# Sorting 200,000 edges in groups of eight tiles: lookup tables by groups of four nodes, one lookup product and sum a group, key rows by broadcast DMA

## The chip, the cores and the metric

The kernel runs on one core of a Trainium2 chip. Times are microseconds (us) on the device for one execution. The time of a kernel is the median of its runs: 11170.59 us here, of three runs between 11164.8 and 11173.62.

## What is computed

Two graph layers stand behind each other on 12,500 nodes with 32 features and 200,000 edges, `src` to `dst`, sorted by `dst` as they come in. The first is a spline convolution whose edge coordinates are moved by a small network (two more spline convolutions, of ones and of 64 hidden features) before it is applied to the features. The second is graph attention with four heads and a GRU cell. Cut to the order of the work:

```python
h = jnp.maximum(_layernorm(x), 0.0)
row, col = src, dst
msg = einsum('es,eso->eo', basis, z[col[:, None] * K + idx])   # K = 125, S = 8
out = segment_sum(msg, row) / max(segment_sum(ones, row), 1) + b
new_pseudo = clip(pseudo + t[col] - t[row], 0, 1)              # t from two such convolutions
x = x + spline_conv(h, row, col, *spline_basis(new_pseudo), W, b)
h = jnp.maximum(_layernorm(x), 0.0)
alpha = softmax over the edges into dst of leaky_relu(el[src] + er[dst])
x = x + elu(GRU(segment_sum(feat[src] * alpha, dst), h))
```

The spline convolutions sum by `src`, so the edges are needed in the order of `src` too. The kernel sorts them itself. The change is in that sort.

## The kernel before

The program is written by hand, engine by engine. It runs through phases, each a block with one instruction stream for each of SP (SyncE, which only issues DMAs here), DVE, ACT, PE and POOL, with semaphores between them. On the profile's clock:

- `constants`, then `load_nodes_and_edges` (L150 to L217) up to 66 us: keys, edge coordinates and features come in. The keys lie as 128 partitions by 1568 tiles, so a **tile** is 128 edges, one a partition. DVE splits each `src` key into its low 7 bits `src_lo` and its high part `src_hi` (0 to 97), makes `c.src`, the key in f32, and builds the records (key, `dst`, three coordinates) that will be sorted.
- `count_and_prefix`, up to about 523 us: counts the edges of each node with one-hot products and makes `c.base`, where the edges of each node start in the sorted order, as a table of 128 (low part) by 98 (high part).
- `sort_edges` (L440 to L612), 524 to 3254 us: it works out the place of each edge and scatters its record there.
- the convolution of ones to about 4040 us, the one of hidden features, two passes of `flow_conv` to about 6600 and 9550 us, the second norm, and the attention to the end. POOL gathers rows by indirect DMAs in the flow phases too (L961, L1614), in steps of 128 rows.

**`sort_edges`** takes the 1568 tiles in 196 groups of G = 8. `u` is the parity of the group g and picks one of two buffers. The place of an edge is the number that stands for its key in the running table (where the next edge of this key goes), plus how many edges before it in its pair of tiles have the same key. For a group:

- DVE makes the one-hots of the *next* group: `rk_lo` (8 x 128, L463) and `rk_hi` (8 x 98, L465).
- PE transposes the eight `rk_lo` one-hots (`turn`, L522), and ACT copies them to SBUF as `rk_lo_t` (`take_lo`, L567).
- So that each edge can be compared with all edges of its pair of tiles, every partition needs the keys of a tile in a row. PE makes them: ACT copies the group's keys to `rk_cols` (L564), and `rows_of` multiplies them, broadcast over 128 columns, by the identity in f32 (L530), into `rk_rows_ps` in PSUM.
- PE goes through the tiles in four pairs, k = 0 to 3. Two products add the one-hots of the pair to the running table `rk_run_ps` in PSUM (L549, bf16, 98 columns). ACT copies it to `rk_table` (L587), in turn in two buffers. Two products look up the pair in the table as it was before the pair (L554, f32, 98 columns): they pick for each edge the row of its low part.
- For every tile, DVE counts the equal keys that stand earlier (L487, one instruction over 128 or 256 elements with a sum at its end). It then waits for the tile's lookup and picks the column of the high part by a product with `rk_hi` and a sum (L492). At the end of the group it adds the two (L497, `rk_place`).
- POOL waits for the place and for ACT's copy of the records (`rk_rec`, L583). It then issues eight indirect DMAs (L609, `rec<-rk_rec,rk_place`), one a tile, each of which writes 128 records of 32 bytes to their places.
- SP stores `feat_table` (L503), then clears `rows4` for a later phase by 112 DMAs of 252 KB each (L506, `rows<-rk_blank`), behind each other and without a wait.

What orders the work is the semaphores. DVE may write `place` when the scatters of group g-2 have landed (`scattered[u]`), ACT `rec` likewise. PE's lookup of tile j waits (L553) until DVE has taken tile j-2, which used the same half of `rk_look_ps`. DVE's one-hots for g+1 wait until PE has added the last pair of g-1, and `rows_of(g + 1)` is issued behind each pair of g. The two waits of DVE and of POOL that the scatters hang on:

```python
dve.wait_ge(looked, g * G + j + 1)                 # before L492, for every tile
...
pool.wait_ge(place_made, g + 3)
pool.wait_ge(rec_ready, g + 1)
```

Of the kernel before, what the change touches and what calls it, by code (L numbers as in the profile page):

```python
# [6 lines left out]
BF16 = mybir.dt.bfloat16  # L7
# [18 lines left out]
NQ = NW // G  # L26
SPREADS = 4
# [124 lines left out]
def load_nodes_and_edges(nc, c, d, sem):  # L152
# [4 lines left out]
    with nc.Block() as block, ExitStack() as ctx:  # L157
        sb, _, _ = allocators(nc, ctx)
        tmp, stat = sb("ln_tmp", [P, NB, FEAT]), sb("ln_stat", [P, 3, NB])
        pseudo = sb("pseudo", [P, NT, 3])  # L160
        keys_stored = sem("in_keys_stored")

        @block.sync
        def _(sp):
# [20 lines left out]
            sp.dma_start(d.dst_key.rearrange("(p t) w -> p (t w)", t=PIECES), c.dst_i[:, :]).then_inc(keys_stored, 16)  # L185
            sp.wait_ge(keys_stored, 32)

        @block.scalar
        def _(act):
            act.wait_ge(var_ready, 1)  # L190
            act.activation(stat[:, 2, :], stat[:, 1, :], ACT.Sqrt).then_inc(std_ready, 1)

        @block.vector
        def _(dve):
# [7 lines left out]
            for a in (c.src, c.src_lo, c.src_hi):  # L202
                chain(dve.memset(a[:, NT:NT + G], 0.0))
# [3 lines left out]
            chain(dve.tensor_copy(c.src[:, 0:NT], c.src_i[:, :]))  # L207
# [5 lines left out]
            chain(dve.tensor_copy(c.rec[:, :, 0:1], c.src[:, 0:NT].unsqueeze(2)))  # L213
# [7 lines left out]
def count_and_prefix(nc, c, d, sem):  # L221
# [6 lines left out]
    with nc.Block() as block, ExitStack() as ctx:  # L228
# [26 lines left out]
        def _(dve):  # L255
# [50 lines left out]
            chain(dve.tensor_copy(off[:, :], first))  # L306
            dve.sem_inc(off_made, 1)
# [111 lines left out]
def sort_edges(nc, c, d, sem):  # L419

    hots_made = sem("rk_hots_made")
    turned = sem("rk_turned")
    lo_ready = sem("rk_lo_ready")
    cols_made = sem("rk_cols_made")
    rows_made = sem("rk_rows_made")
# [3 lines left out]
    sums = sem("rk_sums")  # L433
# [3 lines left out]
    pool_turn = sem("rk_pool_turn")  # L437
    tail_made = sem("rk_tail_made")
    earlier_made = sem("rk_earlier_made")
    blank_made, blank_stored, feat_stored = sem("rk_blank_made"), sem("rk_blank_stored"), sem("rk_feat_stored")  # L440
    with nc.Block() as block, ExitStack() as ctx:
        sb, ps, _ = allocators(nc, ctx)
        lo_hot, hi_hot = sb("rk_lo", [P, 2, G, P], BF16), sb("rk_hi", [P, 2, G, NB], BF16)
        lo_t = sb("rk_lo_t", [P, 2, G, P])
        table = sb("rk_table", [P, 2, NB])
        junk, junk_l = sb("rk_junk", [P, 2, G // 2, 3, P], BF16), sb("rk_junk_l", [P, 2, G, NB], BF16)
# [7 lines left out]
        lo_ps = ps("rk_lo_ps", [P, G, P], BF16)
        rows = ps("rk_rows_ps", [P, 2, G, P])
        look = ps("rk_look_ps", [P, 2, 512])
        run = ps("rk_run_ps", [P, 512])
# [57 lines left out]
        def _(pe):  # L515
# [1476 lines left out]
```

## Time and profile before

| | |
|---|---|
| median of the runs | 11170.59 us (11164.8 to 11173.62) |
| span of the profiled execution | 12528.6 us; it has no time beside its span |
| PE, PEld busy | 6505.4 us (52%), 5397.9 us (43%) |
| DVE busy | 7716.2 us (62%) |
| ACT busy | 2933.1 us (23%) |
| POOL busy | 7476.5 us (60%) |
| DMA | 605.09 MB, 48 GB/s over the span |

The span runs from the first to the last instruction of one execution that the profiler recorded. A busy time is the sum of an engine's instructions. PEld is the loading of PE's weights, beside PE. L487 and the like are lines of the kernel, which stand above with their numbers. A wait is put down to the engine whose semaphore ended it; where the profile finds none, it says "remote" or "issue". One core runs, so nothing is remote in the sense of another core.

### The profile page before, as it was taken

How to read it: one execution, taken by the hardware profiler on the slowest of the kernel's cores; microseconds unless marked ns; L12 is line 12 of the kernel's file. 1: busy time of each engine (PE TensorE's matmuls, PEld its weight loads, DVE VectorE, ACT ScalarE, POOL GpSimd, SP SyncE). 2: the span in 40 equal slices, each digit the busy share in tenths (PEclk: the TensorE clock that was granted, in tenths of full speed). 3: DMA queues.
4: the chain of work that ended last, by engine and by line, in shares of the span. 5: the costliest groups of instructions: out<-in, count | busy, mean ns of one | idle time of the engine just before them, and what ended most of it. 6: DMA issues, size and time to landing. Idle time of an engine off the chain costs nothing. (4 is left out here: it accounts for less than half of the span.)

```text
span 12528.6 us, 178083 instructions
## 1 busy us (share of the span) xinstructions
PE 6505.4 (52%) x38968; PEld 5397.9 (43%) x38968; DVE 7716.2 (62%) x17239; ACT 2933.1 (23%) x8407; POOL 7476.5 (60%) x7456
## 2 busy tenths in 40 slices
PE   3466666666475799999994444545555100000000
PEld 2355555555475677777764434434454100000000
DVE  9844444444498676666664444544576267777777
ACT  0011111111132344344432222322343000000001
POOL 5155555655200888888886888888800566666663
PEclk9966666666698999999997667766777555555555
DMA  1210000000733444444443333333322212221221
GB/s 41 65 36 2 2 2 2 2 2 2 14 41 50 93 93 94 92 94 95 92 93 49 50 51 53 54 50 52 54 42 34 35 49 50 51 50 48 51 54 40
DMA packets 1788557, 605.09 MB, mean 48 GB/s; under 512 B 1595943, under 2 KB 1729575, under 8 KB 1788260
## 3 DMA queue, kind: packets, MB, share of 16 engines
q1 hardware_dynamic: 1078132, 311.05, 12.8%
q0 software_dynamic: 255648, 274.30, 10.7%
q10 hardware_dynamic: 454736, 19.28, 3.0%
q8 instruction: 15, 0.25, 0.0%
q14 instruction: 26, 0.21, 0.0%
HBM read 430.75 MB, written 172.95 MB: 48 GB/s over the span
## 5 line engine op out<-in xcount | busy, mean ns | idle before, releaser
L1222 PE MATMUL c_acc<-c_spread_sb,c_basis_sb 128*125 128x256 f32 (+1 forms) x12544 | 2599.2, 376 | 1502.8 <-issue 655.0
L1222 PEld LDWEIGHTS c_acc<-c_spread_sb,c_basis_sb 128*125 128x125 f32 x12544 | 2266.5, 231 | 1803.5 <-issue 1536.3
L1614 POOL DMA_INDIRECT at_ring<-gat_table,at_place x1568 | 1585.7, 1011 | 1188.5 <-issue 1188.5
L609 POOL DMA_INDIRECT rec<-rk_rec,rk_place x1568 | 1619.3, 1033 | 1110.1 <-DVE rk_place L497 620.7
L1321 ACT ACTIVATE c_sums<-c_acc 125x512 f32<-125x512 f32 (+1 forms) x3136 | 1489.3, 490 | 2258.7 <-PE c_acc L1222 1298.6
L961 POOL DMA_INDIRECT c_ring<-hid_table,c_at x1568 | 1707.1, 1089 | 478.9 <-issue 443.2
L961 POOL DMA_INDIRECT c_ring<-feat_table,c_at x1568 | 1602.7, 1022 | 478.1 <-issue 462.9
L1084 DVE TENSOR_TENSOR c_spread_sb<-c_mark,c_rin 128x512 f32<-128x512 f32 (+1 forms) x3136 | 1745.2, 557 | 60.3
L1871 PE MATMUL gr_hps<-ident,gr_hs 128*32 128x128 f32 x98 | 29.8, 408 | 2473.7 <-issue 2066.3
L492 DVE CUSTOM_DVE_ANT_0 rk_junk_l<-rk_look_ps,rk_hi 128x98 bf16<-128x98 f32 x1568 | 402.2, 257 | 1324.1 <-remote 821.1
L1234 PE MATMUL c_mix<-c_sums,c_w 125*64 125x256 f32 (+1 forms) x9408 | 1037.3, 401 | 187.6 <-issue 133.8
L554 PE MATMUL rk_look_ps<-rk_table,rk_lo_t 128*128 128x98 f32 x3136 | 908.7, 425 | 379.5 <-DVE rk_before L492 327.4
L1871 PEld LDWEIGHTS gr_hps<-ident,gr_hs 128*32 128x32 f32 x98 | 6.4, 109 | 2488.1 <-issue 2078.1
L554 PEld LDWEIGHTS rk_look_ps<-rk_table,rk_lo_t 128*128 128x128 f32 x3136 | 705.4, 292 | 503.3 <-DVE rk_before L492 404.2
L1783 DVE TENSOR_REDUCE at_sums<-at_prod 128x128 f32<-128x5248 f32 x98 | 873.3, 8911 | 24.0 <-issue 14.1
L1234 PEld LDWEIGHTS c_mix<-c_sums,c_w 125*64 125x64 f32 (+1 forms) x9408 | 627.4, 132 | 559.2 <-issue 304.0
L530 PE MATMUL rk_rows_ps<-ident,rk_cols 128*128 128x128 f32 x3152 | 771.1, 390 | 4.7 <-ACT rk_cols L564 4.5
L1110 DVE TENSOR_SCALAR c_rel<-c_rin,first 128x16 f32<-128x16 f32 x392 | 103.3, 264 | 1014.6 <-DMA c_rin<-rows 434.9
L587 ACT ACTIVATE rk_table<-rk_run_ps 128x98 f32<-128x98 f32 x784 | 196.2, 250 | 2173.9 <-PE rk_run_ps L549 1208.1
L530 PEld LDWEIGHTS rk_rows_ps<-ident,rk_cols 128*128 128x128 f32 x3152 | 664.9, 292 | 6.4 <-ACT rk_cols L564 6.4
L1144 DVE SCALAR_TENSOR_TENSOR c_hat<-c_hat,c_sides 128x96 f32<-128x96 f32 x196 | 52.5, 268 | 985.3 <-issue 785.6
L487 DVE SCALAR_TENSOR_TENSOR rk_junk<-rk_rows_ps,src_f,rk_earlier 128x128 bf16<-128x128 f32 (+1 forms) x1568 | 647.2, 413 | 2.0 <-PE rk_rows_ps L530 2.0
(356 smaller groups left out, 10126.9 us busy)
## 6 DMA issues: line engine op xcount, KB each, us to landing
c_rin<-rows SPq DMA_DIRECT2D x3136, 42.0 KB
c_rin<-rows SPq DMA_DIRECT2D x3136, 20.0 KB
rows<-c_ring POOLq DMA_DIRECT2D x392, 128.0 KB
rows<-rk_blank SPq DMA_DIRECT2D x112, 252.0 KB
rows<-c_ring POOLq DMA_DIRECT2D x392, 72.0 KB
rows<-at_ring SPq DMA_DIRECT2D x196, 144.0 KB
rec<-rk_rec,rk_place POOLq DMA_INDIRECT x1568
c_ring<-hid_table,c_at POOLq DMA_INDIRECT x1568
```

The source lines that it names most:

```text
L487: dve.scalar_tensor_tensor(junk[:, u, j // 2, odd:2 * odd + 1, :], rows[:, u, j - odd:j + 1, :], c.src[:, bass.ds(g * G + j, 1)], earlier[ ...
L492: dve.tensor_tensor_reduce(junk_l[:, u, j, :], look[:, j % 2, 0:NB], hi_hot[:, u, j, :], 1.0, 0.0, ALU.mult, ALU.add, before[:, u, j:j + 1 ...
L530: last = pe.matmul(rows[:, u, j, :], bc(cols[:, u, j:j + 1], [P, P]), c.ident[:, :], start=True, stop=True)
L554: pe.matmul(look[:, j % 2, 0:NB], lo_t[:, u, j, :], table[:, k % 2, :], start=True, stop=True).then_inc(looked, 1)
L609: pool.indirect_dma_start(out=d.rec, out_offset=bass.IndirectOffsetOnAxis(ap=place[:, u, j:j + 1], axis=0), in_=rec[:, u, j, :], in_offset ...
L961: pool.indirect_dma_start(out=ring[:, u, j, :], out_offset=None, in_=table, in_offset=bass.IndirectOffsetOnAxis(ap=at[:, h, u, j:j + 1], a ...
L1084: dve.tensor_tensor(spread[:, q, w, :, :], bc(mark[:, q, w, :].unsqueeze(2), [P, 2, feats, WN]), bc(rin[:, q, w, 0:feats].unsqueeze(3), [P ...
L1222: last = pe.matmul(acc[pp % BANKS][:, (w % 2) * WN * feats:(w % 2 + 1) * WN * feats], basis[:, q, w, :, :].rearrange("p a b -> p (a b)"), ...
L1234: last = pe.matmul(mix[k * outs:(k + 1) * outs, 0:2 * P], wsb[:, f, :], sums[:, f, :], start=(i_f == 0), stop=(i_f == each - 1))
L1321: act.activation(sums[:, :, at:at + 2 * WN].rearrange("p f (k n) -> p k f n", n=WN), acc[pp % BANKS][:, 0:pair].rearrange("p (k f n) -> p ...
L1614: pool.indirect_dma_start(out=ring[:, u, j, :], out_offset=None, in_=d.gat_table, in_offset=bass.IndirectOffsetOnAxis(ap=place[:, u, j:j + ...
L1783: dve.tensor_reduce(sums[:, v, :], prod[:, v, :, :, :].rearrange("p s h f -> p (h f) s"), X, ALU.add)\
```

## The change

The running table and the lookups no longer go by node but by **group of four nodes** (WN = 4, as later phases use them): 98 by 32 entries for 128 by 98. The edges come out in the order of their groups of four.

- **Load phase.** `group` (key >> 2, f32) and `group_lo` (the same and 31, bf16) take the place of `c.src`. PE transposes `group` in fourteen steps of 112 tiles, ACT copies them to SBUF, and SP stores them as `group_rows` (1568 x 128) in DRAM: row t holds the 128 groups of tile t. `count_and_prefix` copies the first node of each group out of its table as `group_base`.
- **DVE.** `rk_lo` is 8 x 32. The eight counts (now L508) compare groups and read `rk_rows` from SBUF. In place of eight L492 there are one product over all eight lookups (L519, `rk_found`, 256 elements from PSUM) and one sum (L523, `rk_before`). Behind six counts DVE waits once for `looked`, makes the product, the seventh count, the sum, and the eighth count; then comes the place (L527).
- **PE.** `rows_of` is gone. The transposes are of `rk_hi`, the lookups multiply the transposed `rk_hi` by the table (128 x 32 for 128 x 98), all eight into one bank of 256 columns, one bank for each u. PE waits once a group for DVE (the product of two groups ago), and signals `looked` once, behind the last pair.
- **ACT.** `rk_cols` is gone, `take_hi` takes the place of `take_lo`, `rk_rec` is made at the end of the group, no longer at its start.
- **SP.** A group's rows are loaded by one DMA that reads the eight rows of `group_rows` (4 KB) for all 128 partitions (512 KB land). It waits for DVE's last count of group g-2. The 112 clears go one behind each of the first 112 loads, and `feat_table` is stored behind the clears.
- POOL's stream is the same.

The diff, cut (the same names changed in `constants` of the sizes and in the declarations are left out):

```diff
+            sp.wait_ge(rows_taken, -(-TURNS // 4))
+            sp.dma_start(d.group_rows.rearrange("(k t) p -> t k p", t=TURNED), rows_sb[:, :, :]).then_inc(rows_stored, 16)
...
+            for k in range(TURNS):
+                if k % 4 == 0 and k >= 8:
+                    pe.wait_ge(rows_taken, k // 4 - 1)
+                last = pe.transpose(rows_ps[k // 4 % 2][:, k % 4, :], c.group[:, k * TURNED:(k + 1) * TURNED], c.ident[:, :])
+                if k % 4 == 3 or k == TURNS - 1:
+                    last.then_inc(rows_turned, 1)
...
-            chain(dve.tensor_copy(c.src[:, 0:NT], c.src_i[:, :]))
+            chain(dve.tensor_scalar(c.key_tmp[:, :], c.src_i[:, :], WN_BITS, None, ALU.logical_shift_right))
+            chain(dve.tensor_copy(c.group[:, 0:NT], c.key_tmp[:, :]))
+            dve.sem_inc(grouped, 1)
+            chain(dve.tensor_scalar(c.key_tmp[:, :], c.key_tmp[:, :], NW - 1, None, ALU.bitwise_and))
+            chain(dve.tensor_copy(c.group_lo[:, 0:NT], c.key_tmp[:, :]))
...
+            chain(dve.tensor_copy(c.group_base[:, :], first))
...
-                dve.tensor_tensor(lo_hot[:, u, :, :], bc(c.ramp_bf[:, :].unsqueeze(1), [P, G, P]),
-                                  bc(c.src_lo[:, at].unsqueeze(2), [P, G, P]), ALU.is_equal).then_inc(hots_made, 1)
+                dve.tensor_tensor(lo_hot[:, u, :, :], bc(c.ramp_bf[:, 0:NW].unsqueeze(1), [P, G, NW]),
+                                  bc(c.group_lo[:, at].unsqueeze(2), [P, G, NW]), ALU.is_equal).then_inc(hots_made, 1)
 
...
+                    def count_in_pair(*tiles):
+                        for j in tiles:
+                            odd = j % 2
+                            dve.scalar_tensor_tensor(
+                                junk[:, u, j // 2, odd:2 * odd + 1, :], rows[:, u, j - odd:j + 1, :],
+                                c.group[:, bass.ds(g * G + j, 1)], earlier[:, 1 - odd:2, :], ALU.is_equal, ALU.mult,
+                                accum_out=in_tile[:, u, j:j + 1]).then_inc(ranked, 1)
+
                     dve.wait_ge(updated, g * (G // 2) + 1)
                     hots(g + 1, 1 - u)
-                    dve.wait_ge(rows_made, g + 1)
-
+                    dve.wait_ge(rows_loaded[u], i * 16 + 16)
                     dve.wait_ge(place_made, g + 1)
-                    for j in range(G):
-                        odd = j % 2
-                        dve.scalar_tensor_tensor(
-                            junk[:, u, j // 2, odd:2 * odd + 1, :], rows[:, u, j - odd:j + 1, :],
-                            c.src[:, bass.ds(g * G + j, 1)], earlier[:, 1 - odd:2, :], ALU.is_equal, ALU.mult,
-                            accum_out=in_tile[:, u, j:j + 1]).then_inc(sums, 1)
-                        dve.wait_ge(looked, g * G + j + 1)
-                        dve.tensor_tensor_reduce(junk_l[:, u, j, :], look[:, j % 2, 0:NB], hi_hot[:, u, j, :], 1.0, 0.0,
-                                                 ALU.mult, ALU.add, before[:, u, j:j + 1]).then_inc(sums, 1)
-
-                    dve.wait_ge(sums, (g + 1) * 2 * G + 4)
+                    count_in_pair(*range(first_part))
+                    dve.wait_ge(looked, g + 1)
+                    dve.tensor_tensor(found[:, :, :], look[u][:, 0:G * NW].rearrange("p (j w) -> p j w", w=NW),
+                                      lo_hot[:, u, :, :], ALU.mult).then_inc(ranked, 1)
+                    count_in_pair(first_part)
+                    dve.wait_ge(ranked, (g + 2) * steps + to_product)
+                    dve.tensor_reduce(before[:, :], found[:, :, :], X, ALU.add).then_inc(ranked, 1)
+                    count_in_pair(first_part + 1)
+                    dve.wait_ge(ranked, (g + 3) * steps)
                     dve.wait_ge(scattered[u], i * (16 * G) + 16)
-                    dve.tensor_tensor(place[:, u, :], in_tile[:, u, :], before[:, u, :], ALU.add)\
-                        .then_inc(place_made, 1)
+                    dve.tensor_tensor(place[:, u, :], in_tile[:, u, :], before[:, :], ALU.add).then_inc(place_made, 1)
 
...
+            def load_rows(i, u):
+                sp.wait_ge(ranked, (i * 2 + u) * steps + steps)
+                sp.sem_inc(sp_turn, 1)
+                sp.dma_start(rows[:, u, :, :].rearrange("p g n -> p (g n)"),
+                             bc(d.group_rows[bass.ds((i * 2 + u) * G, G), :].rearrange("g n -> (g n)").unsqueeze(0),
+                                [P, G * P])).then_inc(rows_loaded[u], 16)
+
+            def clear(k):
                 sp.dma_start(rows_v[bass.ds(k, 1), :, :].rearrange("k p w -> (k p) w"),
                              blank[:, :, :].rearrange("p t w -> p (t w)")).then_inc(blank_stored, 16)
+
+            sp.wait_ge(blank_made, 1)
+            with sp.Fori(0, NT // BLANK // 2) as i:
+                for u in range(2):
+                    load_rows(i, u)
+                    clear(i * 2 + u)
+            sp.dma_start(node_view(d.feat_table, 36)[:, :, 0:FEAT], c.h[:, :, :]).then_inc(feat_stored, 16)
...
+                    pe.wait_ge(ranked, g * steps + to_product)
                     for k in range(G // 2):
 
-                        pe.wait_ge(lo_ready, g * 4 + k + 1)
                         pe.wait_ge(table_ready, g * (G // 2) + k + 1)
-
                         for j in (2 * k, 2 * k + 1):
-                            last = pe.matmul(run[:, 0:NB], lo_hot[:, u, j, :], hi_hot[:, u, j, :],
+                            last = pe.matmul(run[:, 0:NW], hi_hot[:, u, j, :], lo_hot[:, u, j, :],
                                              start=False, stop=True, skip_group_check=True)
                         last.then_inc(updated, 1)
+                        pe.wait_ge(hi_ready, g * (G // 2) + k + 1)
                         for j in (2 * k, 2 * k + 1):
-                            pe.wait_ge(sums, g * 2 * G + 2 * j + 2)
-                            pe.matmul(look[:, j % 2, 0:NB], lo_t[:, u, j, :], table[:, k % 2, :],
-                                      start=True, stop=True).then_inc(looked, 1)
+                            last = pe.matmul(look[u][:, j * NW:(j + 1) * NW], hi_t[:, u, j, :], table[:, k % 2, :],
+                                             start=True, stop=True)
+                        if k == G // 2 - 1:
+                            last.then_inc(looked, 1)
                         if k == 1:
                             turn(g + 1, 1 - u)
-                        rows_of(g + 1, 1 - u, k)
 
...
-                    act.wait_ge(rows_made, g + 1)
-                    take_cols(g + 1, 1 - u)
-
-                    act.wait_ge(scattered[u], i * (16 * G) + 16)
-                    act.activation(rec[:, u, :, :], c.rec[:, bass.ds(g * G, G), :], ACT.Copy).then_inc(rec_ready, 1)
...
+                            take_hi(1 - u, 2 * k - 4)
+                            take_hi(1 - u, 2 * k - 3)
+                    act.wait_ge(scattered[u], i * (16 * G) + 16)
+                    act.activation(rec[:, u, :, :], c.rec[:, bass.ds(g * G, G), :], ACT.Copy).then_inc(rec_ready, 1)
 
```

PE, at the head of its loop over pairs of groups, before: L540 is the loop's head, L553 the wait for `sums`, once for each lookup, L545 the wait for `lo_ready`.

```order
L540 UNCONDITIONAL_BRANCH
L540 ISA
L549 MATMUL rk_run_ps<-rk_hi,rk_lo 128x98 x2
L553 ISA
L554 MATMUL rk_look_ps<-rk_table,rk_lo_t 128x98
L553 REGISTER_ALU
L554 MATMUL rk_look_ps<-rk_table,rk_lo_t 128x98
L528 REGISTER_ALU
L530 MATMUL rk_rows_ps<-ident,rk_cols 128x128 x2
L545 REGISTER_ALU
```

PE, the same place in the changed kernel.

```order
L572 UNCONDITIONAL_BRANCH
L572 ISA
L578 ISA
L580 MATMUL rk_run_ps<-rk_lo,rk_hi 98x32 x2
L585 MATMUL rk_look_ps<-rk_table,rk_hi_t 128x32 x2
L578 REGISTER_ALU
L580 MATMUL rk_run_ps<-rk_lo,rk_hi 98x32 x2
L585 MATMUL rk_look_ps<-rk_table,rk_hi_t 128x32 x2
L563 ISA
```

The two products of a pair are back to back, the waits between them and the L530 behind them are gone.

DVE, from the second one-hot of the loop on, before. Each tile has its wait for `looked` (L491).

```order
L465 TENSOR_TENSOR rk_hi<-ramp_bf,src_hi 128x784
L487 ISA
L487 SCALAR_TENSOR_TENSOR rk_junk,rk_in_tile<-rk_rows_ps,src_f,rk_earlier 128x128
L491 REGISTER_ALU
L492 ISA rk_junk_l,rk_before<-rk_look_ps,rk_hi 128x98
L492 ISA rk_before 128x1
L487 ISA
L487 SCALAR_TENSOR_TENSOR rk_junk,rk_in_tile<-rk_rows_ps,src_f,rk_earlier 128x256
L491 REGISTER_ALU
L492 ISA rk_junk_l,rk_before<-rk_look_ps,rk_hi 128x98
L492 ISA rk_before 128x1
```

DVE, the end of a group in the changed kernel, from the sixth count on.

```order
L508 ISA
L508 SCALAR_TENSOR_TENSOR rk_junk,rk_in_tile<-rk_rows,group_f,rk_earlier 128x128
L508 ISA
L508 SCALAR_TENSOR_TENSOR rk_junk,rk_in_tile<-rk_rows,group_f,rk_earlier 128x256
L519 TENSOR_TENSOR rk_found<-rk_look_ps,rk_lo 128x256
L508 ISA
L508 SCALAR_TENSOR_TENSOR rk_junk,rk_in_tile<-rk_rows,group_f,rk_earlier 128x128
L522 ISA
L523 TENSOR_REDUCE rk_before<-rk_found 128x8
L508 ISA
L508 SCALAR_TENSOR_TENSOR rk_junk,rk_in_tile<-rk_rows,group_f,rk_earlier 128x256
L525 ISA
```

One product and one sum stand for the eight L492, and the two last counts stand between them and behind them.

SP, its loop before and then the changed one. L505 is a Fori over 112; L536 is the load of the rows, L541 the clear, L534 the wait for `ranked`.

```order
L505 ISA
L506 DMA rows<-rk_blank 128x504
L505 REGISTER_ALU
L505 COMPARE_AND_BRANCH
L508 DMA rows<-rk_blank 128x36
```

```order
L545 ISA
L536 ISA
L536 DMA rk_rows<-group_rows 128x1024
L541 ISA
L541 DMA rows<-rk_blank 128x504
L534 ISA
L536 ISA
L536 DMA rk_rows<-group_rows 128x1024
L541 ISA
L541 DMA rows<-rk_blank 128x504
```

Every clear has a load ahead of it, and a wait ahead of the load.

## Rows read from the trace of the kernel before

**Rows 1.** Cores view: the core, its span, TensorE's mean granted clock.

```profile
core 0: 12528.6 us, clock 0.721
```

**Rows 2.** Page, busy; windows view: us, PE PEld DVE ACT POOL, clock, DMA, GB/s.

```profile
PE 6505.4 (52%) x38968; PEld 5397.9 (43%) x38968; DVE 7716.2 (62%) x17239; ACT 2933.1 (23%) x8407; POOL 7476.5 (60%) x7456
...
530.00:3254.00 2724.00, 1753.57 (x9415) 1558.39 (x9413) 1314.88 (x6858) 462.70 (x1960) 1618.65 (x1568) 0.64 0.06 13
```

**Rows 3.** Source view of L497: min/median/max ns, first and last start, shape.

```profile
L497 DVE TENSOR_TENSOR rk_place<-rk_in_tile,rk_before x196: 166/167/169, 536.3 to 3241.7; 128x8 uint32<-128x8 f32 x196
```

**Rows 4.** Waits view, 1400 to 3400 us: total us, times, longest.

```profile
ACT rk_table L587 <- remote: 621.7, 130, 7.0
...
POOL rec L609 <- DVE rk_place L497: 434.9, 128, 3.6
```

**Rows 5.** Timeline, one group: start us, duration, instruction, idle before it.

```profile
2010.73 1.27 POOL L609 DMA_INDIRECT rec<-rk_rec,rk_place  x1 [3.43 <-DVE rk_place L497]
...
2017.48 0.37 PE L549 MATMUL rk_run_ps<-rk_hi,rk_lo 128*128 128x98 bf16 x2
...
2019.96 0.97 POOL L609 DMA_INDIRECT rec<-rk_rec,rk_place  x1 [0.30 <-issue]
2022.30 0.25 ACT L587 ACTIVATE rk_table<-rk_run_ps 128x98 f32<-128x98 f32 x1 [5.61 <-remote]
2022.35 0.26 DVE L492 CUSTOM_DVE_ANT_0 rk_junk_l<-rk_look_ps,rk_hi 128x98 bf16<-128x98 f32 x1 [3.81 <-remote]
...
2023.23 0.17 DVE L497 TENSOR_TENSOR rk_place<-rk_in_tile,rk_before 128x8 uint32<-128x8 f32 x1
...
2024.29 1.68 POOL L609 DMA_INDIRECT rec<-rk_rec,rk_place  x1 [3.35 <-DVE rk_place L497]
```

**Rows 6.** Timeline, group 0, before POOL's first scatter.

```profile
530.91 0.35 DVE L487 SCALAR_TENSOR_TENSOR rk_junk<-rk_rows_ps,src_f,rk_earlier 128x128 bf16<-128x128 f32 x1 [2.01 <-PE rk_rows_ps L530]
...
531.18 0.26 DVE L492 CUSTOM_DVE_ANT_0 rk_junk_l<-rk_look_ps,rk_hi 128x98 bf16<-128x98 f32 x1
...
531.36 0.48 DVE L487 SCALAR_TENSOR_TENSOR rk_junk<-rk_rows_ps,src_f,rk_earlier 128x256 bf16<-128x256 f32 x1
...
531.77 0.25 DVE L492 CUSTOM_DVE_ANT_0 rk_junk_l<-rk_look_ps,rk_hi 128x98 bf16<-128x98 f32 x1
...
535.97 0.25 PE L549 MATMUL rk_run_ps<-rk_hi,rk_lo 128*128 128x98 bf16 x2
...
536.55 0.23 ACT L587 ACTIVATE rk_table<-rk_run_ps 128x98 f32<-128x98 f32 x1
```

**Rows 7.** Lines view by form, DVE, 1400-3240 us: busy us, mean ns, idle before.

```profile
L463 DVE TENSOR_TENSOR rk_lo<-ramp_bf,src_lo 128x1024 bf16<-128x1024 bf16 x133 | 162.9, 1225 | 37.9 <-issue 31.9 <-PE rk_run_ps L549 0.5
L465 DVE TENSOR_TENSOR rk_hi<-ramp_bf,src_hi 128x784 bf16<-128x784 bf16 x133 | 128.7, 968 | 0.0
```

**Rows 8.** Lines view of PE by form, the same stretch.

```profile
L530 PE MATMUL rk_rows_ps<-ident,rk_cols 128*128 128x128 f32 x2128 | 521.4, 390 | 2.5 <-ACT rk_cols L564 2.3
```

**Rows 9.** DMA view, 530 to 700 us, where the clears run.

```profile
DMA packets 27459, 30.45 MB, mean 179 GB/s; under 512 B 13104, under 2 KB 27440, under 8 KB 27456
```

**Rows 10.** DMA view, 30 to 76 us, in 40 slices of 1.15 us.

```profile
GB/s 83 118 146 145 145 143 144 145 145 138 287 436 415 291 0 0 0 0 0 0 0 0 0 0 0 0 0 0 0 0 0 0 0 0 0 0 0 0 0 0
```

**Rows 11.** Windows view, second flow convolution, with POOL's gathers and without.

```profile
8000.00:8900.00 900.00, 457.89 (x2769) 372.69 (x2768) 430.77 (x1057) 256.30 (x803) 722.20 (x764) 0.70 0.33 52
9100.00:9500.00 400.00, 238.58 (x1872) 213.35 (x1865) 282.46 (x691) 175.54 (x533) 0.00 (x0) 0.79 0.24 42
```

**Rows 12.** Timeline of DVE in the load phase.

```profile
34.37 0.98 DVE L209 TENSOR_SCALAR key_tmp<-src_i 128x1568 int32<-128x1568 int32 x1
...
64.43 1.79 DVE L145 TENSOR_SCALAR h<-h 128x3136 f32<-128x3136 f32 x1
```

**Rows 13.** Timeline in the second flow convolution.

```profile
8310.64 2.44 DVE L1100 TENSOR_TENSOR c_basis_sb<-c_plane,c_hat 128x1000 f32<-128x1000 f32 x2
8311.33 1.33 POOL L961 DMA_INDIRECT c_ring<-feat_table,c_at  x1 [0.31 <-issue]
```

More of the change, by code:

```diff
@@ L161, in load_nodes_and_edges @@
         keys_stored = sem("in_keys_stored")
+        grouped, rows_turned, rows_taken, rows_stored = (
+            sem(f"in_{x}") for x in ("grouped", "rows_turned", "rows_taken", "rows_stored"))
+        rows_ps = [ps(f"in_rows{k}", [TURNED, 4, P]) for k in range(2)]
+        rows_sb = sb("in_rows_sb", [TURNED, TURNS, P])
         @block.sync
@@ L201, in _ @@
             dve.sem_inc(cleared, 1)
-            for a in (c.src, c.src_lo, c.src_hi):
+            for a in (c.group, c.group_lo, c.src_lo, c.src_hi):
                 chain(dve.memset(a[:, NT:NT + G], 0.0))
@@ L426, in sort_edges @@
     turned = sem("rk_turned")
-    lo_ready = sem("rk_lo_ready")
-    cols_made = sem("rk_cols_made")
-    rows_made = sem("rk_rows_made")
+    hi_ready = sem("rk_hi_ready")
+    rows_loaded = [sem(f"rk_rows_loaded{u}") for u in range(2)]
     looked = sem("rk_looked")
@@ L440, in sort_edges @@
     blank_made, blank_stored, feat_stored = sem("rk_blank_made"), sem("rk_blank_stored"), sem("rk_feat_stored")
+    first_part = 6
+    to_product, to_sum, steps = first_part + 1, first_part + 3, G + 2
     with nc.Block() as block, ExitStack() as ctx:
         sb, ps, _ = allocators(nc, ctx)
[L443 to L446, printed above, removed]
+        lo_hot, hi_hot = sb("rk_lo", [P, 2, G, NW], BF16), sb("rk_hi", [P, 2, G, NB], BF16)
+        hi_t = sb("rk_hi_t", [NB, 2, G, P])
+        table = sb("rk_table", [NB, 2, NW])
+        rows = sb("rk_rows", [P, 2, G, P])
+        junk, found = sb("rk_junk", [P, 2, G // 2, 3, P], BF16), sb("rk_found", [P, G, NW])
         earlier = sb("rk_earlier", [P, 2, P])
-        in_tile, before = sb("rk_in_tile", [P, 2, G]), sb("rk_before", [P, 2, G])
+        in_tile, before = sb("rk_in_tile", [P, 2, G]), sb("rk_before", [P, G])
         place = sb("rk_place", [P, 2, G], U32)
         rec = sb("rk_rec", [P, 2, G, ROW])
-        cols = sb("rk_cols", [P, 2, G])
         tail = sb("rk_tail", [P, 2, TAIL // P // 2 * ROW])
         blank = sb("rk_blank", [P, BLANK, GW])
[L454 to L457, printed above, removed]
+        hi_ps = ps("rk_hi_ps", [NB, G, P], BF16)
+        look = [ps(f"rk_look_ps{u}", [P, 512]) for u in range(2)]
+        run = ps("rk_run_ps", [NB, 512])
         @block.vector
@@ L510, in _ @@
                 .then_inc(blank_stored, 16)
+            with sp.Fori(NT // BLANK // 2, NG // 2) as i:
+                for u in range(2):
+                    load_rows(i, u)
             sp.wait_ge(blank_stored, (NT // BLANK + 2) * 16)
@@ L570, in _, with take_hi @@
-            take_cols(0, 0)
+            def take_hi(u, q):
+                act.activation(hi_t[:, u, 2 * q:2 * q + 2, :], hi_ps[:, 2 * q:2 * q + 2, :], ACT.Copy).then_inc(hi_ready, 1)
             act.wait_ge(updated, 1)
-            act.activation(table[:, 0, :], run[:, 0:NB], ACT.Copy).then_inc(table_ready, 1)
+            act.activation(table[:, 0, :], run[:, 0:NW], ACT.Copy).then_inc(table_ready, 1)
             act.wait_ge(turned, 1)
-            for q in range(4):
-                take_lo(0, q)
+            for q in range(G // 2):
+                take_hi(0, q)
```

53 lines of the change are left out of this document (23 added, 30 removed).

## The prediction

> **What bounds the kernel now.** I first take the cores view for the span: 12528.6 us on one core [rows 1]. No view gives a time of that execution beyond its span, so the sum is made against the span. It is 1358 us (12%) above the 11170.59 us median of the runs. That gap matters below: a wait that I see may be shorter, or absent, in an execution that is not profiled.
>
> Then the windows view, for the one stretch that the change rebuilds: 530 to 3254 us, 2724 us [rows 2]. No engine is full in it: POOL is busy 1619 us, PE 1754, DVE 1315, ACT 463, and DMA moves 13 GB/s. The source view of the place instruction gives the beat: 196 of them, the first at 536.3 and the last at 3241.7, so 2705.4 / 195 = **13.87 us a group** [rows 3].
>
> What sets 13.87? The waits view names POOL waiting for DVE's `rk_place`, and ACT for its table with "remote" as the releaser [rows 4]. The timeline shows both [rows 5]. POOL issues a group's eight scatters from 2010.73 to 2020.93 (the last starts at 2019.96). PE issued its last table update, L549, at 2017.48, and it should be done by 2017.85. But ACT's copy, which needs nothing else, starts at 2022.30, and DVE, which waits for the lookup of tile 6, goes on at 2022.35. Both come 1.4 us behind the end of POOL's eighth issue. Tiles 6 and 7 end, the place is made at 2023.23, and POOL starts again at 2024.29. So the loop is serial: burst 10.2, release 1.4, tail 2.0, together 13.6. I call the middle part the **hold**: PE's last results reach the others only when POOL's burst is over, 3.8 to 4.4 us late.
>
> The hold is neither DVE's nor PE's work. In group 0, before POOL's first issue, the lookups went from 531.18 to the place at 536.3 [rows 3] in 5.1 us, and ACT's copy at 536.55 stood 0.3 behind the end of its L549 (535.97 + 0.25) [rows 6]. With the one-hots (1.23 and 0.97 us [rows 7]) and the first count (0.27, from 530.91) that is a group in 7.6 us.
>
> **POOL's own beat.** An issue takes 0.97 us and 0.30 lies before it, 1.27; the first of a burst, beside DVE's L463 and L465, takes 1.27 or 1.68 [rows 5]. Eight slots are 8.9 + 1.6 to 8.9 + 2.0, so 10.5 to 10.9, and I take **10.7**. The 1568 scatters are the same before and after: by this trace no version goes below 8 x 1.27 = 10.2 a group.
>
> **The change part by part**, each 196 times.
> - DVE, one-hots: 1024 elements take 1225 ns, 784 take 968 [rows 7], so 1.07 ns an element and 0.40 us for the new 256: -0.8.
> - DVE, lookups: eight L492, 0.18 us each from its start to the next L487 [rows 6], go: -1.4. An L487 pair takes 0.27 + 0.41 to the lookups' starts [rows 6], four pairs 2.7, so of the 5.1 us another 1.0 was waiting for PE, and goes too. A product of 256 elements from PSUM comes (98 took 0.26 [rows 6], 158 more at 1.07: 0.43) and a reduce of 256 (0.4). Eight waits on `looked` become one.
> - DVE, same-key counts: eight L487 stay. They read `rows` from SBUF now. DVE's group is 7.6 - 0.8 - 2.4 + 0.8 = 5.2 us.
> - PE: L530 goes (16 records a group, busy 521.4 us in 133 groups, 3.9 each), L554 and L549 stream 32 columns for 98; 9415 records are 48 a group [rows 2, 8], afterwards 32. From 1754 / 196 = 8.9 us a group PE comes to some 4 to 5.
> - ACT: `cols` goes, tables shrink, four big copies stay; it was busy 463 / 196 = 2.4 us. No bound.
> - SP: a broadcast load of 512 KB a group is new, and for the first 112 groups a 252 KB clear is issued behind it. The clears alone ran at 179 GB/s [rows 9], so 2.9 us and with the clear 4.4. The load waits for `ranked` of group g-2 and has all of g-1 to land; at the slowest slice of the load phase, 83 GB/s [rows 10], 6.3 us still fit under 10.7. I cost it at nothing: POOL's burst is its cover. The other end is the 42 GB/s of a late stretch [rows 11], if 128 reads of one 4 KB source were so slow: 12.5 us a group, and then it is the bound.
> - Load phase: three more DVE passes over 1568 elements at 0.98 [rows 12], **+3.1 us** on the path. The fourteen transposes and the 784 KB store are free: DMA is idle from 46 us on [rows 10] and DVE's last step there ends at 66.2 [rows 12]. One small copy in the count phase: +0.2. `feat_table` is stored behind the clears, at about 1800 us, and is first read long after the sort: nothing.
>
> **The sum.** In a profiled execution: 13.87 - 10.7 = 3.17 us, x 196 = -621, + 3.3 = **-618 us**, if the hold sets the place no more. I expect that, since it took only the last ten of PE's 48 matmul records, and 32 remain.
>
> In the runs the gain lies between this and nothing. Late PE results and POOL's indirect transfers go together: in the second flow convolution PE starts 2769 / 900 = 3.1 matmuls a us with POOL at work, and 1872 / 400 = 4.7 once POOL is done, in the same code [rows 11]. If only the profile made the hold, the sort would run at POOL's beat already. I share the 1358 us by POOL's busy time, 1619 of 7476.5 us in the sort [rows 2]: 294 us, 1.5 a group. The group before is then 12.4 us in the runs, the gain 1.7 x 196 = 333, less 3: **-330, 10,840 us**. No row is nearer to either end, so I take the share.
>
> **A rule that speaks against it.** L487's large operand moves from PSUM to SBUF, so two tensors come from SBUF. Beside L487 and L492 POOL's issue stayed at 0.97. Beside L463 and L465, with two SBUF inputs, it took 1.27 to 1.68 [rows 5], and beside the f32 products of L1100 1.33 [rows 13].
> The Trainium skill ("Advanced Engine Details and Errata", VectorE Performance Modes) says that Vector's second SBUF port is shared with GpSimd, and that two-port Vector modes and GpSimd instructions block each other. [...]
>
> **Rivals.**
> 1. *Slower: POOL's beat before and after, and the port.* It needs runs without the hold; the 1358 us speak for that, but they may lie elsewhere too. The price is then POOL's: L487's 2.7 us a group touch about three issues, at +0.2 to +0.36 each 0.6 to 1.1 us, less 0.3 for the shorter L463. +0.3 to +0.8, x 196 = +60 to +160 us: 11,270. It decides once the group before is under 11 us in the runs.
> 2. *The hold stays.* The product waits for all eight tiles. If PE's last result still comes 1.4 us behind POOL's burst, more stands behind it: product, count, reduce, count, place, 1.7 us for 1.05 now. +0.65, x 196 = +127: 11,300. For it: the release follows POOL and not PE's work. Against: PE has a third fewer records.
> 3. *No change.* No hold in the runs and no port: POOL paces both, 11,174.
>
> **How the numbers follow.** A measurement of this kernel can tell 0.2%, 22 us. Forecast (60 to 618 us faster): 0.54, its own range 10,550 to 11,110. Rival 1: 0.24, rival 2: 0.08, rival 3: 0.14. So faster 0.54, same 0.14, slower 0.32. The range goes from the forecast's far end into rivals 1 and 2, 10,560 to 11,290, and leaves out a slow broadcast load.
>
> **What would show it.** Right: places 10.5 to 11 us apart, POOL's pause between bursts under 1 us, DVE idle at its wait for `scattered`, `rk_rows` landed before DVE wants it, the sort near 2100 us. Wrong: POOL still waits 3 us for `rk_place` (rival 2), POOL's mean issue over 1.1 us for 1.03 (rival 1), or DVE waits for `rk_rows`. If the span falls by 600 us and the runs do not, the hold was the profile's, and what fails is the step that shares the 1358 us.

## The result, and the profile after

The changed kernel takes 11089.99 us (median of 4 runs, 11075.97 to 11105.63) against 11172.1 us for the kernel before: a ratio of 0.993, 95% interval 0.9918 to 0.9942, some 80 us faster. Measured again, it was 0.9933 (0.992 to 0.9947). The forecast was 10,840.

The span of the profiled execution is now the time of the runs, which that of before was not ([rows 1]: 12528.6 us). The cores view:

```profile
core 0: 11092.1 us, clock 0.808
```

The page's busy times, and the windows view of the sort (PE, PEld, DVE, ACT, POOL busy, clock, DMA share, GB/s), which answer to [rows 2]:

```profile
PE 5597.3 (50%) x35830; PEld 4756.7 (43%) x35830; DVE 7359.3 (66%) x14500; ACT 2935.8 (26%) x8215; POOL 7507.0 (68%) x7456
```

```profile
530.00:2630.00 2100.00, 1042.81 (x6280) 996.43 (x6278) 974.04 (x4116) 410.02 (x1768) 1575.02 (x1568) 1.00 0.24 67
```

The source view of the place, L527, which was L497:

```profile
L527 DVE TENSOR_TENSOR rk_place<-rk_in_tile,rk_before x196: 166/167/240, 537.8 to 2601.0; 128x8 uint32<-128x8 f32 x196
```

Places stand (2601.0 - 537.8) / 195 = 10.58 us apart, where [rows 3] had 13.87. From the first place to the last it is 2063.2 us for 2705.4, 642 less, a little more than the 621 of the sum, and the runs are only 80 shorter. PE is busy 1043 us in the sort for 1754, DVE 974 for 1315, and it is not they that the time hangs on (the 1754 are of the long execution; the second profile below has 1338 and 1309). The waits view of the sort, and the group of POOL's scatters in the lines view (busy us, mean ns, idle before and its causes):

```profile
ACT rk_rec L615 <- DMA rec<-rk_rec,rk_place: 1132.9, 194, 11.3
...
DVE rk_place L527 <- DMA rec<-rk_rec,rk_place: 818.7, 192, 9.7
...
POOL rec L632 <- issue: 477.9, 1470, 4.2
...
POOL rec L632 <- DVE rk_place L527: 20.9, 36, 10.3
```

```profile
L632 POOL DMA_INDIRECT rec<-rk_rec,rk_place x1568 | 1575.0, 1004 | 517.8 <-issue 478.3 <-DVE rk_place L527 20.9 <-ACT rk_rec L615 18.6
```

DVE and ACT wait for POOL's transfers (819 and 1133 us), and POOL waits 21 us in all for a place. So POOL sets the pace, issue behind issue (10.3 of the 21 us lie before its first issue). And `rk_rows` is there in time: DVE waited for it once, 2.0 us.

### The profile page after: what moved, and what is told of

The parts are those of the page before. It is cut to its first block and busy times, and to the rows that moved or that the text cites. A ratio compares the mean times of both kernels' runs of the same rounds, so it can differ in the third digit from the quotient of the medians.

```text
span 11092.1 us, 165912 instructions
## 1 busy us (share of the span) xinstructions
PE 5597.3 (50%) x35830; PEld 4756.7 (43%) x35830; DVE 7359.3 (66%) x14500; ACT 2935.8 (26%) x8215; POOL 7507.0 (68%) x7456
## 5 line engine op out<-in xcount | busy, mean ns | idle before, releaser
L1637 POOL DMA_INDIRECT at_ring<-gat_table,at_place x1568 | 1656.4, 1056 | 701.4 <-issue 701.1
L632 POOL DMA_INDIRECT rec<-rk_rec,rk_place x1568 | 1575.0, 1004 | 517.8 <-issue 478.3
L1257 PE MATMUL c_mix<-c_sums,c_w 125*64 125x256 f32 (+1 forms) x9408 | 867.0, 380 | 24.6 <-ACT c_sums L1344 24.6
L585 PE MATMUL rk_look_ps<-rk_table,rk_hi_t 98*128 98x32 f32 x3136 | 808.5, 401 | 0.4 <-ACT rk_hi_t L595 0.4
L580 PE MATMUL rk_run_ps<-rk_lo,rk_hi 128*98 128x32 bf16 x1568 | 257.5, 244 | 1014.4 <-ACT rk_table L608 1014.4
L585 PEld LDWEIGHTS rk_look_ps<-rk_table,rk_hi_t 98*128 98x128 f32 x3136 | 761.1, 333 | 0.5 <-ACT rk_hi_t L595 0.5
L1257 PEld LDWEIGHTS c_mix<-c_sums,c_w 125*64 125x64 f32 (+1 forms) x9408 | 543.2, 128 | 313.5 <-ACT c_sums L1344 34.7
L580 PEld LDWEIGHTS rk_run_ps<-rk_lo,rk_hi 128*98 128x98 bf16 x1568 | 220.7, 197 | 1040.4 <-ACT rk_table L608 1040.4
L991 POOL DMA_DIRECT2D rows<-c_ring x784 | 626.7, 799 | 11.3 <-DMA c_ring<-hid_table,c_at 5.8
L1797 DVE TENSOR_TENSOR at_prod<-at_weight,at_run 128x1280 f32<-128x1280 f32 x392 | 583.9, 1489 | 10.1
L508 DVE SCALAR_TENSOR_TENSOR rk_junk<-rk_rows,group_f,rk_earlier 128x128 bf16<-128x128 f32 (+1 forms) x1568 | 575.9, 413 | 2.0 <-DMA rk_rows<-group_rows 2.0
```

What stands on the lines that cost most here:

```text
L508: dve.scalar_tensor_tensor(junk[:, u, j // 2, odd:2 * odd + 1, :], rows[:, u, j - odd:j + 1, :], c.group[:, bass.ds(g * G + j, 1)], earlie ...
L585: last = pe.matmul(look[u][:, j * NW:(j + 1) * NW], hi_t[:, u, j, :], table[:, k % 2, :], start=True, stop=True)
L632: pool.indirect_dma_start(out=d.rec, out_offset=bass.IndirectOffsetOnAxis(ap=place[:, u, j:j + 1], axis=0), in_=rec[:, u, j, :], in_offset ...
L991: pool.dma_start(rows_v[:, bass.ds(t * tiles + u * slot, slot), :], ring[:, u, :, :]).then_inc(stored[u], 16)
L1257: last = pe.matmul(mix[k * outs:(k + 1) * outs, 0:2 * P], wsb[:, f, :], sums[:, f, :], start=(i_f == 0), stop=(i_f == each - 1))
L1637: pool.indirect_dma_start(out=ring[:, u, j, :], out_offset=None, in_=d.gat_table, in_offset=bass.IndirectOffsetOnAxis(ap=place[:, u, j:j + ...
```

## The experiments

### The kernel before, profiled again, and the changed one again

No edit.

> The kernel before, unchanged, profiled once more. The runs say 82 us between the two kernels, so 85 us of sort once the load phase's 3 are taken off, 0.43 us a group; the changed kernel's group is 10.58 us. Theory A (the hold belongs to the one execution that was profiled, not to the runs): the span is near 11170 us, places stand 11.0 us apart, and ACT's copies of the table follow their L549 within 1 us. Theory B (the profiler makes the hold each time in this kernel): the span is again near 12,500 us and the places 13.9 us apart, though the runs take 11170.

One run: 11177.9 us. The cores view, the source view of the place, and POOL's scatters in the lines view:

```profile
core 0: 11176.1 us, clock 0.765
```

```profile
L497 DVE TENSOR_TENSOR rk_place<-rk_in_tile,rk_before x196: 166/168/230, 537.5 to 2667.7; 128x8 uint32<-128x8 f32 x196
```

```profile
L609 POOL DMA_INDIRECT rec<-rk_rec,rk_place x1568 | 1639.6, 1046 | 517.4 <-issue 467.9 <-DVE rk_place L497 36.1 <-ACT rk_rec L583 13.5
```

Theory A. The span is the time of the runs and a group takes (2667.7 - 537.5) / 195 = 10.92 us. The hold of [rows 5] is in none of the other eleven profiles of this study, all of whose spans lie within 10 us of the runs: ACT's copies of the table begin 0.04 us (the median) behind the end of PE's last table update in each of them, and 0.50 us in the profile with the hold. What made it in that one execution stays open.

POOL set the pace before the change too: 36 us in the whole sort are put down to a place, not 435 in two thirds of it [rows 4], and of these 90 times 86 are only the 0.30 us that lie before every issue. POOL really waited for a place four times, 1.7 to 3.2 us, in the first nine groups. But its issues took 1046 ns on average, and 1004 after. That is 1568 x 42 ns = 65 us, and the places' stretch fell by 2130.2 - 2063.2 = 67.0. All of the sort's gain is in the length of POOL's issues. Where are the long ones? Three issues from the timeline of this profile, with the one-hots that DVE runs beside them:

```profile
2002.70 1.23 DVE L463 TENSOR_TENSOR rk_lo<-ramp_bf,src_lo 128x1024 bf16<-128x1024 bf16 x1
...
2002.92 1.85 POOL L609 DMA_INDIRECT rec<-rk_rec,rk_place  x1 [0.30 <-DVE rk_place L497]
...
2003.84 0.97 DVE L465 TENSOR_TENSOR rk_hi<-ramp_bf,src_hi 128x784 bf16<-128x784 bf16 x1
...
2013.98 0.96 POOL L609 DMA_INDIRECT rec<-rk_rec,rk_place  x1 [0.30 <-DVE rk_place L497]
...
2014.16 1.23 DVE L463 TENSOR_TENSOR rk_lo<-ramp_bf,src_lo 128x1024 bf16<-128x1024 bf16 x1 [0.49 <-issue]
...
2024.06 1.22 DVE L463 TENSOR_TENSOR rk_lo<-ramp_bf,src_lo 128x1024 bf16<-128x1024 bf16 x1
...
2024.17 1.96 POOL L609 DMA_INDIRECT rec<-rk_rec,rk_place  x1 [0.30 <-DVE rk_place L497]
...
2025.20 0.97 DVE L465 TENSOR_TENSOR rk_hi<-ramp_bf,src_hi 128x784 bf16<-128x784 bf16 x1
```

All three are the seventh issue of a burst; the 0.30 us that the profile puts down to the place lie before every issue. The first and the last begin while L463 runs, and end 0.93 us after it has made room for L465 (2004.77 and 2026.13, against 2003.84 and 2025.20). They wait for its end and then take about their usual 0.97. The middle one began 0.18 us before L463 and is not touched. This gives a new theory, the **lock**: I went through all 1568 issues of this profile and asked what DVE ran when each began. 202 began inside L463 or L465, and these took 121 us more than 0.969 each. 157 of them waited over 0.05 us, 0.77 on average, and 156 of these took longer by what was left of the one-hot less 0.12 to 0.13 us; the other 45 began in the first 0.06 or the last 0.19 us of it. 636 began inside L487 or L492, which have an input from PSUM, and took nothing more. In the second profile of the changed kernel the one-hots cost 39 us and the counts, now with both tensors in SBUF, 20.

The Trainium skill ("SBUF — State Buffer", SBUF: two separate sides) says this: the port pair that Vector and GpSimd share is an exclusive lock, not a share of the bandwidth; whichever starts first has it for its whole instruction, and a Vector operation with two SBUF inputs counts among them against a GpSimd operation that reads SBUF. For POOL's issues the trace agrees, with the 157 waits above. It shows no Vector instruction held in turn: the middle L463 began 0.18 us behind an issue and took its usual 1.23, and none of the 197 took over 1.30.

Which issues met the one-hots? L463 follows right behind a place. In this profile a place was ready 0.9 to 5.4 us (median 2.9) before the burst that uses it, so L463 ran beside the end of the burst before: the sixth, seventh and eighth issues of a burst waited 17, 57 and 76 times, the first 7 times. In the long execution of [rows 5] each place released a burst, and there it was the first issue that waited, 195 times, 97 us in all.

> The changed kernel, unchanged, as the yardstick of this call: 11090 us, 0.993 of before, group 10.58 us. Theory B would let its profile, too, show a hold now and then, with a span some hundred us above the runs.

11106.11 us, ratio 0.9933, group 10.60 us, span 11103.9: as expected.

### Counts from PSUM, and every count twice

```diff
+                    dve.wait_ge(rows_made, g + 1)
...
+                    pe.wait_ge(ranked, (g + 2) * steps)
+                    rows_of(g + 1, 1 - u)
```

> The changed kernel, but the counts (L508) read the key rows from PSUM again: ACT copies the groups' columns, PE makes the rows by eight f32 products at the end of a group. The broadcast load stays and lands in a buffer nobody reads. Port theory (rival 1: DVE's counts with two SBUF inputs hold up POOL's issues): POOL's mean issue falls from 1.004 to about 0.98 us and the group from 10.58 to 10.3, 50 us faster than the changed kernel. POOL theory (the counts' operand does not matter): within 20 us of the changed kernel, issues 3 to 6 of a burst stay at 1.0 to 1.1 us. PE's extra 3.4 us a group are hidden under 10.5 in both.

```diff
+                            dve.scalar_tensor_tensor(
+                                junk2[:, u, j // 2, odd:2 * odd + 1, :], rows[:, u, j - odd:j + 1, :],
+                                c.group[:, bass.ds(g * G + j, 1)], earlier[:, 1 - odd:2, :], ALU.is_equal, ALU.mult,
+                                accum_out=in_tile2[:, u, j:j + 1]).then_inc(ranked, 1)
```

> The changed kernel with every count made twice, the second into a buffer nobody reads: DVE's group grows by 2.7 us to about 8, still under 10.58. Port theory: two more issues of each burst stand beside counts from SBUF, the group grows by 0.1 to 0.4 us, 20 to 80 us slower than the changed kernel. POOL theory: no change, within 20 us.

Measured: 0.992 (0.9907 to 0.9934) with the rows from PSUM, 14 us under the 11106.11 of the changed kernel beside it. 0.9951 (0.9938 to 0.9965) with every count twice, 19 us over it. POOL's scatters in the two:

```profile
L649 POOL DMA_INDIRECT rec<-rk_rec,rk_place x1568 | 1570.2, 1001 | 518.6 <-issue 486.1 <-ACT rk_rec L632 17.2 <-DVE rk_place L531 15.3
```

```profile
L637 POOL DMA_INDIRECT rec<-rk_rec,rk_place x1568 | 1593.5, 1016 | 518.4 <-issue 464.4 <-DVE rk_place L532 30.0 <-ACT rk_rec L620 24.0
```

The port theory had the sign both times and was too dear: 14 us for 50, and 19 for 20 to 80. But both times also lie within the 20 us that the POOL theory allowed, and the interval of the first overlaps that of the changed kernel (0.992 to 0.9947), so the times alone do not decide. The issues do: none of the 405 that began inside a count from PSUM waited, and with every count twice the counts cost 46 us for 20. With the rows from PSUM the issues waited longer at the one-hots (51 us for 39), so only 8 of the 20 us were saved. A count is short (0.35 or 0.48 us), and an issue that meets one waits for the rest of that one only.

### The ramp in PSUM, and the low one-hot wide again

```diff
+        ramp = ps("rk_ramp_ps", [P, 512])
...
-                dve.tensor_tensor(hi_hot[:, u, :, :], bc(c.ramp_bf[:, 0:NB].unsqueeze(1), [P, G, NB]),
+                dve.tensor_tensor(hi_hot[:, u, :, :], bc(ramp[:, 0:NB].unsqueeze(1), [P, G, NB]),
```

> The changed kernel with the ramp that both one-hots are compared with in PSUM (f32): the same two instructions, of about the same length, but with one input from SBUF. Lock theory (an issue of POOL that starts while DVE runs an instruction with two SBUF inputs waits for that instruction's end, and an input from PSUM takes no part): of the 59 us that the issues wait in the changed kernel (39 at the one-hots L488 and L490, 20 at the counts) the 39 go. Ratio to before 0.9935 - 0.0035 = 0.990, group 10.4 us. Work theory (POOL waits for DVE's work, not for its port): the one-hots are no shorter, 0.993 stays.

Ratio 0.9908 (0.9891 to 0.9924). The instruction is as long as before, 963 ns for 968, and POOL's issues are shorter:

```profile
L491 DVE TENSOR_TENSOR rk_hi<-rk_ramp_ps,src_hi 128x784 bf16<-128x784 f32 x111 | 106.9, 963 | 0.0
```

```profile
L634 POOL DMA_INDIRECT rec<-rk_rec,rk_place x1568 | 1545.0, 985 | 519.2 <-issue 473.3 <-ACT rk_rec L617 24.1 <-DVE rk_place L529 21.8
```

Not one of the 177 issues that began inside a one-hot waited over 0.05 us. The work theory falls here: the same work of the same length, with one input elsewhere, is 1578.0 - 1545.0 = 33 us less of POOL's time than in the changed kernel's second profile (30 less than in its first). The size was 33 and not 39, since the counts took 26 us of waits for 20.

TensorE's clock can be ruled out here too. In the windows view of this kernel's sort the granted clock was 0.50 (1.2 GHz), against 1.00 (2.4 GHz) in the changed kernel's profile above, and the sort was shorter all the same.

```diff
-                dve.tensor_tensor(lo_hot[:, u, :, :], bc(c.ramp_bf[:, 0:NW].unsqueeze(1), [P, G, NW]),
-                                  bc(c.group_lo[:, at].unsqueeze(2), [P, G, NW]), ALU.is_equal).then_inc(hots_made, 1)
+                dve.tensor_tensor(lo_hot[:, u, :, :], bc(c.ramp_bf[:, :].unsqueeze(1), [P, G, P]),
+                                  bc(c.group_lo[:, at].unsqueeze(2), [P, G, P]), ALU.is_equal).then_inc(hots_made, 1)
```

> The changed kernel with the low one-hot 128 wide again (L488 1.23 us for 0.42), of which 32 columns are used; everything else, PE's lost work, the one lookup product, the broadcast load, stays. Lock theory: issues are 1.27 us apart, so 0.87 of the groups have one that starts in the 1.1 us of L488 and waits 0.55 on average, +0.43 us a group, 85 us slower than the changed kernel: 11,180, the time of before. Work theory: DVE's group is 0.8 longer but far under 10.6: no change from the changed kernel.

```profile
L632 POOL DMA_INDIRECT rec<-rk_rec,rk_place x1568 | 1610.3, 1027 | 523.8 <-issue 462.9 <-ACT rk_rec L615 39.4 <-DVE rk_place L527 21.4
```

Ratio 0.9969 (0.9957 to 0.998), 1610.3 - 1575.0 = 35 us more of issues. The sign is the lock's, the size under half of my 85 us. I had let issues begin at any time. They don't: 128 issues, in 196 groups, waited at L488, 80 us in all, but the issues then met the counts at another phase: 391 still began inside a count, only 30 of them waited (284 of 405 in the changed kernel), and the 20 us shrank to 4. So of the change's 65 us, more than half is the narrower one-hot as such. The other 29 us lie between the wide one-hot and the kernel before, where 157 issues waited 0.77 us on average at a one-hot, for 142 and 0.61 here. What sets that timing was not isolated.

### The kernel before with one-input one-hots

```diff
-                dve.tensor_tensor(lo_hot[:, u, :, :], bc(c.ramp_bf[:, :].unsqueeze(1), [P, G, P]),
-                                  bc(c.src_lo[:, at].unsqueeze(2), [P, G, P]), ALU.is_equal).then_inc(hots_made, 1)
+                for j in range(G):
+                    dve.tensor_scalar(lo_hot[:, u, j, :], c.ramp_bf[:, :], lo_f[:, bass.ds(g * G + j, 1)], None,
+                                      ALU.is_equal).then_inc(hots_made, 1)
```

(and the same for `hi_hot`, with the two keys copied to f32 ahead of the loop, and PE's wait for sixteen instructions in place of two.)

> The kernel before with its two one-hots made by sixteen instructions over one tile each that compare the ramp with a number per partition: one tensor from SBUF, some 0.1 to 0.15 us each. Nothing else of the change is in it: node tables, rows by PE, a lookup sum per tile. Lock theory: the 121 us that the issues wait at L463 and L465 go down to some 10 at most, ratio 0.990, 11,070, below the changed kernel. Work theory (the gain came from the work that PE and DVE lost): no faster than before, slower by what sixteen instructions cost.

Ratio 0.990 (0.9884 to 0.9917), and 0.9892 (0.9878 to 0.9905) when measured again, faster than the changed kernel, with nothing of the change in it. Its cores view, its place, its scatters:

```profile
core 0: 11057.8 us, clock 0.769
```

```profile
L502 DVE TENSOR_TENSOR rk_place<-rk_in_tile,rk_before x196: 166/167/242, 545.2 to 2556.4; 128x8 uint32<-128x8 f32 x196
```

```profile
L614 POOL DMA_INDIRECT rec<-rk_rec,rk_place x1568 | 1521.0, 970 | 524.3 <-issue 465.3 <-DVE rk_place L502 36.4 <-ACT rk_rec L588 22.5
```

The issues take 970 ns, and 1521.0 us is what 1568 of them cost without a wait. The 118.6 us that are gone from POOL are the 2130.2 - 2011.2 = 119.0 us that are gone between the first and the last place. DVE did not get faster by it. The new instructions took 0.28 us each, not 0.1 to 0.15, and DVE was busy 1412 us in the sort for 1309 in the second profile of the kernel before. The windows view with the sixteen one-hots:

```profile
530.00:2580.00 2050.00, 1329.82 (x9427) 1255.94 (x9425) 1412.39 (x9600) 484.42 (x1964) 1520.99 (x1568) 0.80 0.08 18
```

### Both cures in the changed kernel

> The changed kernel with the one-hots made by the same sixteen instructions. Lock theory: as with the ramp in PSUM, 0.990, or, if these instructions hold the port too, a few us more, since each is short. Both together with the kernel before in that form within 20 us: then the group tables and the broadcast rows are worth nothing in this loop.

Ratio 0.9914 (0.9898 to 0.9931). The one-hots cost no wait, the counts 35 us, more than the 20 before. It is 14.5 us over the kernel before in the same form, inside the 20 that I had allowed. From the first place to the last it takes 30.5 us longer, which the counts' waits account for. The profiled executions differ by 22.9 us; the rest of the gap between 30.5 and 14.5 lies outside this stretch and between one execution and the next, and was not traced.

Then with the rows from PSUM as well, beside the kernel before with one-input one-hots once more:

> The kernel before with its one-hots by sixteen one-input instructions once more, as the yardstick of this call: ratio 0.990 again, mean issue 0.970 us.

> The changed kernel with both cures: key rows from PSUM and one-hots by sixteen instructions, so that no instruction of DVE in the loop has two inputs from SBUF but the place itself; group tables, one lookup product and the rest of the change stay. Lock theory: mean issue 0.970, POOL at its own pace of 1.274 us a scatter, the same time as the kernel before with only the one-hots altered, within 10 us, ratio 0.990. Work theory: the lighter PE and DVE of the group tables should then show, 20 us or more below it.

```profile
L654 POOL DMA_INDIRECT rec<-rk_rec,rk_place x1568 | 1521.2, 970 | 520.6 <-issue 469.8 <-ACT rk_rec L637 35.6 <-DVE rk_place L536 15.1
```

Both 0.9892: 11072.94 and 11073.8 us. With no lock left in either, group tables and node tables take the same time. What the change takes off PE and DVE is worth nothing here.

In all nine kernels POOL's extra time and the longer stretch agree within 4 us. Each row: POOL's busy time in the sort, what it has above 1521.0, and the stretch from the first to the last place above the last kernel's 2011.2.

| kernel | POOL busy | above | stretch above | ratio |
|---|---|---|---|---|
| before (second profile) | 1639.6 | 118.6 | 119.0 | 1 |
| wide one-hot | 1610.3 | 89.3 | 92.5 | 0.9969 |
| counts twice | 1593.5 | 72.5 | 69.7 | 0.9951 |
| changed | 1575.0 | 54.0 | 52.0 | 0.993 |
| changed, rows in PSUM | 1570.2 | 49.2 | 47.0 | 0.992 |
| changed, 16 one-hots | 1554.8 | 33.8 | 30.5 | 0.9914 |
| changed, ramp in PSUM | 1545.0 | 24.0 | 23.4 | 0.9908 |
| changed, both cures | 1521.2 | 0.2 | -0.9 | 0.9892 |
| before, 16 one-hots | 1521.0 | 0 | 0 | 0.990, again 0.9892 |

## Why the prediction was wrong

**The step that failed** is the share of the 1358 us by POOL's busy time: "The group before is then 12.4 us in the runs". It was 10.92. The 1358 us were all that one execution's own, and no part of the hold was in the runs. I had named this end ("If only the profile made the hold, the sort would run at POOL's beat already") and its sign in the result: the span falls by 600 us and the runs do not. The span fell by 12528.6 - 11092.1 = 1436 us.

**A second step** failed with it. With 10.92 in place of 12.4 the same sum gives (10.92 - 10.7) x 196 = 43, less 3: 40 us faster, half of the measured 82. The other half lies in POOL's beat, which the sum takes as one fixed number, 10.7, before and after, while it fell from 10.92 to 10.58 with its issues.

The other number of the sum, -621 us for the profiled execution, came close to the 642 measured from place to place, and that is luck. It credits the change with ending the hold. The kernel before, profiled again, has no hold either, and the change is worth 67 of the 642.

**What held.** POOL's beat was forecast at 10.5 to 10.9, measured 10.58. Eight scatters at 1.27 are the floor. Its pauses between bursts (0.30 us), the wait of DVE for `scattered` and the rows landed in time came as described. The load phase and the small copy cost 3.5 us (the sort's first instruction on DVE stands at 527.10 for 523.59), forecast 3.3. The broadcast load cost nothing.

**Rival 1** had the condition right (a group before under 11 us) and the sign wrong. It charged L487's move to SBUF with 0.6 to 1.1 us a group: about three issues at 0.2 to 0.36 each. Measured were 2.1 issues a group at 0.05 each, 0.10 a group or 20 us in all, since each instruction of a count can hold an issue only for its own rest. And it credited the shorter L463 with 0.3, where the one-hots' waits fell from 121 to 39 us, 0.42 a group. I charged every issue beside the counts the same sum; the cost is the rest of the one instruction in which an issue begins. The long issues stood in [rows 5] (1.27 and 1.68 beside L463), and I carried them as a fixed 1.6 to 2.0 of POOL's beat, the same before and after, and did not ask what they would be with a shorter L463. That was the gain. Even the place of the long issue was the long execution's own: in the second profile of the kernel before the first issue of a burst took 0.98 us on average, in the changed kernel 0.97, and the long ones came later in the burst.

**Rival 2** did not come: the product never waited for a burst's end. **Rival 3**, POOL pacing both, was right about the pace, and missed the lock.

The section of the Trainium skill that I weighed ("Advanced Engine Details and Errata", VectorE Performance Modes) names two-port modes alone. The counts cost 20 us, so it did not settle the matter; the passage of the Trainium skill on SBUF that stands above has the clause on two SBUF inputs.

**What stays open.** The sort gives 67 of the 75 to 82 us. The rest lies in later phases, whose code is the same. There one profile differs from the next by more than that: from the last scatter of the sort to the next phase's first gather it was 804.5 us in the kernel before, and 788.8 and 801.0 in the changed kernel's two profiles.

## What to carry to other kernels

Compare a profile's span with the runs before reading waits from it. Where they differ by 12%, take a second profile; a wait that fills the difference may belong to that execution alone. Where POOL's indirect DMAs set the pace, look at what DVE runs when each begins: a long instruction with two inputs from SBUF holds it until its end, and one operand in PSUM, or several one-input instructions, removed the wait here without making DVE faster.

## What was not expected of the hardware

An issue of an indirect DMA on POOL took 0.97 us whatever DVE had in hand, unless it began inside a DVE instruction with two SBUF tensors. Then it took the rest of that instruction, less some 0.13 us, on top of its 0.97, up to 2.01 us in all. Both `tensor_tensor` and `scalar_tensor_tensor` with a sum did it. A `tensor_scalar` from SBUF to SBUF in bf16, of 98 or 128 elements, did not: of the 389 issues that began inside one in the kernel before in that form, two took over 50 ns more, and none over 67. Once in 14 groups, from the 28th on, POOL paused 1.5 to 4.5 us behind the first issue of a burst, in every kernel. With a few pauses at the sort's start that is 26 to 35 us. Its cause was not looked for.
